# Causal attention on one core: the tail of one graph and the rows of the next in other places among the 16 items

## The reference

```python
h = _rmsnorm(x, ln1_w)
q = (h @ wq.T).reshape(Bx, Tx, NH, HD).transpose(0, 2, 1, 3)
k = (h @ wk.T).reshape(Bx, Tx, NKV, HD).transpose(0, 2, 1, 3)
v = (h @ wv.T).reshape(Bx, Tx, NKV, HD).transpose(0, 2, 1, 3)
q = q * cos + _rotate_half(q) * sin
k = k * cos + _rotate_half(k) * sin
scores = jnp.einsum('bhtd,bhsd->bhts', q, k) / jnp.sqrt(jnp.float32(HD))
scores = jnp.where(causal[None, None], scores, jnp.float32(-1e+30))
att = jax.nn.softmax(scores, axis=-1)
y = jnp.einsum('bhts,bhsd->bhtd', att, v).transpose(0, 2, 1, 3).reshape(Bx, Tx, Cx)
x = x + y @ wo.T
```

## Time and profile before

| | |
|---|---|
| time, median of 3 runs | 4995.22 us (4994.98 to 4999.32) |
| the profiled execution | 4982.11 us |
| its span | 4980.0 us |
| granted TensorE clock, mean | 0.818 |
| busy PE, DVE, ACT, POOL | 74%, 58%, 40%, 36% of the span |
| this stage | from 3842 to 4578 us of the span |

### The profile page before, as it was taken

One profiled execution on the slowest core, in us unless ns is written; L12 is line 12 of the kernel. 1 busy time (PEld: TensorE's weight loads), 2 busy tenths in 40 slices (PEclk: granted clock), 3 DMA queues, 4 the chain that ended last, 5 costly groups with the idle time before them and its releaser, 6 DMA issues. The chain is left out here.

```text
span 4980.0 us, 82349 instructions
## 1 busy us (share of the span) xinstructions
PE 3668.2 (74%) x24205; PEld 2239.0 (45%) x24205; DVE 2889.9 (58%) x10948; ACT 1986.3 (40%) x4974; POOL 1803.9 (36%) x2183
## 2 busy tenths in 40 slices
PE   3999985566666569999886766489667777764995
PEld 1333333444444323333364555357455444442663
DVE  5666655555555656666487867622377454543444
ACT  1666652222222236666432255334355433332221
POOL 3444421000000044445262136735545234342445
PEclk9999995555555579999998887699889988885997
DMA  4333319300000043333000022144431000001445
GB/s 125 115 113 103 103 50 419 143 0 0 0 0 0 0 130 106 111 106 95 13 0 1 1 89 76 38 133 148 145 101 52 1 9 14 14 17 45 130 130 162
DMA packets 237330, 378.21 MB, mean 76 GB/s; under 512 B 24832, under 2 KB 157056, under 8 KB 228672
## 3 DMA queue, kind: packets, MB, share of 16 engines
q1 hardware_dynamic: 218688, 337.44, 21.3%
q0 software_dynamic: 18432, 38.31, 2.2%
HBM read 210.70 MB, written 164.95 MB: 75 GB/s over the span
## 5 line engine op out<-in xcount | busy, mean ns | idle before, releaser
L1428 DVE CUSTOM_DVE_ANT_0 mha_seen<-mha_score,mha_mask 128x512 f32<-128x512 f32 x1024 | 686.6, 688 | 456.8 <-PE mha_score L1199 453.8
L1331 ACT ACTIVATE mha_prob<-mha_turned 128x512 f32<-128x512 f32 x1024 | 608.9, 601 | 491.8 <-PE mha_turned L1210 461.5
L1592 PE MATMUL lstm_gates<-lstm_h_part,lstm_w_part 128*128 128x16 f16 x4608 | 277.5, 179 | 338.2 <-DVE lstm_h_part L1779 338.2
L3071 POOL DMA_INDIRECT expert_rows<-expert_y,expert_target x320 | 307.1, 960 | 369.1 <-DVE expert_y L3217 155.4
L1199 PE MATMUL mha_score<-mha_k_rows,mha_q_rows 96*128 96x512 bf16 x1024 | 397.0, 390 | 56.9 <-DVE mha_low L1428 28.4
L1592 PEld LDWEIGHTS lstm_gates<-lstm_h_part,lstm_w_part 128*128 128x128 f16 x4608 | 215.7, 107 | 484.3 <-DVE lstm_h_part L1779 482.2
L1209 PE MATMUL mha_turned<-mha_maskT,core_ident_bf 128*128 128x512 bf16 x1024 | 393.3, 384 | 4.2 <-ACT mha_prob L1331 3.5
L1210 PE MATMUL mha_turned<-mha_q_rows,mha_k_rows 99*128 99x512 bf16 x1024 | 391.4, 382 | 0.0
L1542 POOL TENSOR_TENSOR core_mid<-lstm_hist,lstm_per_unit 128x128 f32 x64 | 29.3, 458 | 876.6 <-DVE lstm_hist L1780 876.6
L879 DVE CUSTOM_DVE_ANT_0 mha_prob<-mha_score,mha_mask 128x384 f32<-128x384 f32 (+3 forms) x256 | 125.0, 488 | 306.6 <-PE mha_score L518 222.2
L690 ACT ACTIVATE mha_prob<-mha_prob,mha_bias 128x384 f32<-128x384 f32 (+3 forms) x256 | 143.6, 561 | 361.3 <-DVE mha_bias L879 344.0
(11 more groups left out here) (559 smaller groups left out, 9055.4 us busy)
## 6 DMA issues: line engine op xcount, KB each, us to landing
routed_rows<-lstm_blank SPq DMA_DIRECT2D x66, 1056.0 KB, 27.0
core_params<-adj SPq DMA_DIRECT2D x32, 1024.0 KB, 5.6
gat_adj_raw<-adj SPq DMA_DIRECT2D x32, 1024.0 KB, 5.4
mha_q_rows<-split_rows SPq DMA_DIRECT2D x64, 384.0 KB, 4.3
mha_k_rows<-split_rows SPq DMA_DIRECT2D x64, 384.0 KB, 5.2
expert_x<-routed_rows SPq DMA_DIRECT2D x80, 264.0 KB
expert_w<-weights SPq DMA_DIRECT2D x80, 256.0 KB
combine_pair<-expert_rows SPq DMA_DIRECT2D x32, 512.0 KB, 4.9
```

The costliest lines, as they stand in the source:

```text
L1331: act.activation(prob[:, n % RING, :], turned[n % 2][:, :], ACT.Exp, scale=-1.0).then_inc(S["prob_ready"], 1)
L1428: dve.tensor_tensor_reduce(seen[n % 2][:, :], score[n % 2][:, :], mask[1 - s][:, t, :], 1.0, 3e38, ALU.add, ALU.min, low[g][:, t, j:j + 1] ...
L1592: return pe.matmul(out, w[:, g * P:(g + 1) * P], h_part[:, part, :], start=False, stop=stop, skip_group_check=True)
L3071: pool.indirect_dma_start(out=core.y_rows[NUMBER][:, :], out_offset=bass.IndirectOffsetOnAxis(ap=target[q][:, t:t + 1], axis=0), in_=y_buf ...
```

## The change

For this stage the steps get other items; `values` stays at 3.

| step | before | after |
|---|---|---|
| rows of the next graph | 9 | 0 |
| early (projections, rotations) | 10, 12 | 2, 4 |
| values of the graph before | 3 | 3 |
| back | 4 | 6 |
| ctx | 6 | 9 |
| out | 7 | 11 |
| v | 8, for this graph | 12, for the next graph |
| finish (DVE) | one piece each at 9 to 14 | two pieces each at 13, 14, 15 |

`v32` is held twice, so that v of the next graph can be made while values of this one are still to come; v of graph 0 is made ahead of the loop. POOL normalises the rows of graph b+1 behind its adds for graph b instead of ahead of its adds for b+1. The mask is one strip of 128 x 512, of which each tile reads another part, in place of 4 tiles of 512. Four small buffers that this form of the stage doesn't use are dropped.

```diff
-            at = {"values": 3, "back": 4, "ctx": 6, "out": 7, "v": 8, "rows": 9, "early": (10, 12)}
+            at = {"rows": 0, "early": (2, 4), "values": 3, "back": 6, "ctx": 9, "out": 11, "v": 12}
...
-        mask = [m.sb(f"mask{s}", [P, T, N], BF16) for s in range(1 if rope else 2)]
+        causal = m.sb("causal", [P, N], BF16) if rope else None
+        mask = [] if rope else [m.sb(f"mask{s}", [P, T, N], BF16) for s in range(2)]
...
-        v32 = m.sb("v32", [P, T, heads, 32])
+        v32 = [m.sb(f"v32{s}", [P, T, heads, 32]) for s in range(2)]
...
-                pool.memset(mask[0][:, :, :], 0.0).then_inc(S["adj_zero"], 1)
+                pool.memset(causal[:, :], 0.0).then_inc(S["adj_zero"], 1)
...
-                pool.affine_select(out=mask[0][:, :, :], in_=mask[0][:, :, :], compare_op=ALU.is_ge, fill=BIG, base=0,
-                                   pattern=[[P, T], [-1, N]], channel_multiplier=1).then_inc(S["adj_free"], 1)
+                pool.affine_select(out=causal[:, :], in_=causal[:, :], compare_op=ALU.is_ge, fill=BIG, base=(T - 1) * P,
+                                   pattern=[[-1, N]], channel_multiplier=1).then_inc(S["adj_free"], 1)
+
+            def normalise(b):
+
+                pool.wait_ge(S["xT_ready"], b + 1)
+                pool.tensor_tensor(xn[b % 2][:, :, :], core.mid[:, b], over_features(core.rms[:, b]), ALU.mult)\
+                    .then_inc(S["xn_ready"], 1)
...
+                    if b >= 4:
+                        pool.wait_ge(S["r_scaled"], (b - 2) // 2)
...
+            normalise(0)
             for b in range(B + 5):
                 if b < B:
                     graph(b, b % 2, first=b == 0)
+                if b + 1 < B:
+                    normalise(b + 1)
...
             def project_v(b):
 
+                pe.wait_ge(S["qk_ready"], 4 * b + 4 + 1)
...
-            def back_rows(b):
-
+            def back_rows(b, behind=True):
+
+                if behind:
+                    pe.wait_ge(S["qk_ready"], 4 * (b + 2) + 4 + 1)
...
-                    if n == at["v"]:
-                        project_v(b)
+                    if n == at["v"] and not last:
+                        project_v(b + 1)
...
-            dve.memset(v32[:, :, :, :], 0.0).then_inc(S["v32_set"], 1)
-            dve.wait_ge(S["v32_set"], 1)
...
-                        if 0 <= n - at["out"] - 2 < 6:
-                            finish(b - 1, n - at["out"] - 2)
-                    if n == at["v"] + 1:
-                        take_v(b)
+                        if n >= items - 3:
+                            finish(b - 1, 2 * (n - items + 3))
+                            finish(b - 1, 2 * (n - items + 3) + 1)
+                    if n == at["v"] + 1 and not last:
+                        take_v(b + 1, 1 - s)
```

More of the change, by code:

```diff
@@ L327, in mha_stage @@
         items = 4 * T * groups
-        rstd, shift = m.sb("rstd", [P, B, T]), m.sb("shift", [P, B, T])
-        scratch, term = m.sb("scratch", [P, B, T]), m.sb("term", [P, B, T])
+        rstd, shift, scratch, term = ((None,) * 4 if rope else
+                                      [m.sb(n, [P, B, T]) for n in ("rstd", "shift", "scratch", "term")])
         spare = Spare(core, k)
         adj_raw = None if rope else spare.sb([P, T, N], I32)
-        mask = [m.sb(f"mask{s}", [P, T, N], BF16) for s in range(1 if rope else 2)]
+        causal = m.sb("causal", [P, N], BF16) if rope else None
+        mask = [] if rope else [m.sb(f"mask{s}", [P, T, N], BF16) for s in range(2)]
         xn = [spare.sb([P, T, D]) for s in range(2)]
@@ L481, in project @@
                     pe.wait_ge(S["xT_ready"], b + 1 + 2)
-                    if rope:
-                        pe.wait_ge(S["batch_free"], b + 1)
+                    if rope and (not isinstance(b, int) or b):
+                        pe.wait_ge(S["batch_free"], b)
                 elif n == 2 and not rope:
@@ L528, in transposes, with values @@
                 last.then_inc(S["prob_free"], 1)
-            def values(b, g):
+            def values(b, g, s):
                 done = b * (items // 2) + 2 * T * (g + 1) + 1
@@ L539, in values @@
                         first = u * P if rope else 0
-                        last = pe.matmul(o_ps[g][32 * j:32 * j + 32, first:], v32[:, u, 4 * g + j, :], probT[:, j, u, first:],
+                        last = pe.matmul(o_ps[g][32 * j:32 * j + 32, first:], v32[s][:, u, 4 * g + j, :], probT[:, j, u, first:],
                                          start=(u == 0), stop=(u == T - 1))
                 last.then_inc(S["pv_done"], 1)
-            def back_rows(b):
+            def back_rows(b, behind=True):
+                if behind:
+                    pe.wait_ge(S["qk_ready"], 4 * (b + 2) + 4 + 1)
                 for g in range(groups):
@@ L567, in graph @@
                     if n == at["values"] and not first:
-                        values(b - 1, groups - 1)
+                        values(b - 1, groups - 1, 1 - s)
                     if n == at["values"] + 4 * T:
-                        values(b, 0)
+                        values(b, 0, s)
                     if n >= LAG:
@@ L576, in graph @@
                         if n == at["back"]:
-                            back_rows(b - 1)
+                            back_rows(b - 1, not last)
                         if n == at["ctx"]:
@@ L621, in _ @@
             early(0, 1)
+            project_v(0)
             if sym:
@@ L626, in _ @@
                 transposes(B - 1, n)
-            values(B - 1, groups - 1)
-            back_rows(B - 1)
+            values(B - 1, groups - 1, (B - 1) % 2)
+            back_rows(B - 1, False)
             turn_ctx(B - 1)
@@ L746, in _ @@
                 dve.wait_ge(S["adj_free"], 1)
-            else:
-                dve.memset(v32[:, :, :, head_dim:head_dim + 1], 1.0).then_inc(S["v32_set"], 1)
             def copy_probT(b, n):
@@ L774, in rotate, with take_v @@
                         .then_inc(S["qk_ready"], 1)
-            def take_v(b):
+            def take_v(b, s):
                 dve.wait_ge(S["v_done"], b + 1)
@@ L779, in take_v @@
                 if rope:
[L780 removed]
+                    dve.tensor_copy(v32[s][:, :, :, :], got).then_inc(S["v_ready"], 1)
                 else:
[L782 removed]
+                    dve.tensor_tensor(v32[s][:, :, :, 0:head_dim], got,
                                       bv.rearrange("p (h d) -> p h d", h=heads).unsqueeze(1).broadcast_to([P, T, heads, head_dim]),
@@ L876, in graph @@
                     dve.wait_ge(S["prob_free"], items * b + n + 1)
-                    allowed = mask[0] if rope else mask[s]
                     width = keys(t) * P
-                    dve.tensor_tensor_reduce(prob[:, n % PR, 0:width], score[n % 2][:, 0:width], allowed[:, t, 0:width], 1.0, 3e38,
+                    allowed = causal[:, N - width:N] if rope else mask[s][:, t, 0:width]
+                    dve.tensor_tensor_reduce(prob[:, n % PR, 0:width], score[n % 2][:, 0:width], allowed, 1.0, 3e38,
                                              ALU.add, ALU.min, bias[:, n % PR:n % PR + 1])\
@@ L910, in _ @@
                 rotate(0, 1)
+                take_v(0, 0)
             if sym:
```

3 lines of the change are left out of this document (removed).

## The result

| | before | after |
|---|---|---|
| time, median of 4 runs each | 4995.1 us (4991.2 to 4999.3) | 4879.8 us (4877.1 to 4882.6) |
| ratio, 95% interval | | 0.977 (0.975 to 0.979) |
| the profiled execution | 4982.1 us | 4878.5 us |

Faster by 115 us; 4870 us was forecast, with a range of 4835 to 4905, and 4879.8 lies in it. In the stage of the change the profiled executions give 112.7 us (from the first memset of DVE in the stage to the first operation of POOL in the next, 732.9 us before and 620.3 after). The profiled execution of after enters the stage some 10 us later, in parts that the change does not touch, so the profiled pair as a whole differs by only 103.6 us.

The account below looks back on a forecast made before the run. No engine was full; PE's in-order waits, the lower clock after them and the pause bound the stage. Savings of 29 (graphs 0-4), 90 (5-14), 2.5 (start) and 3 (graph 15) gave 124.5 us, ratio 0.975, 4870 us, range 4835 to 4905.

Parts of the forecast that it names:

- PE's seven stops: In graph 2, PE stops at seven places, 7.7 us in all, each step one or two items behind what it needs.
- The floor of 23.0 us: PE's work in graph 2: 35.7 us less 7.7 of waits and 5.0 lost to the lower clock.
- Graphs without routing: Graphs before the scatter begins: 27.3 us at full clock, 27.5 us with a partly low clock, against 35.7.
- next graph's first score waits for it: Items 12 to 15 hold 7.5 us of DVE work against PE's 4.5 + 0.9, costing 2.1 us a graph.
- Even graphs: Graphs 4, 6 to 14 with routing: DVE's extra work adds 1.3 + 3.2 us, giving 32 us, without the pause.
- pause: At values, ACT's copy comes 8.1 us after their start under a scatter, 2.9 without; 5.3 us stays in odd graphs.
- the lumps: Even graphs' 7.3 us of extra DVE work, at items 0 to 3 and 6 to 7, priced at 1.3 + 3.2 us.
- Odd graphs: Graphs 5, 7 to 13 with routing: 27.5 + 2.2 routing + 5.3 pause + 0.5 for scales = 35.5 us.
- B: Rival: from some point a scatter holds all PE work, not values alone; 50 us more, 4920 us; chance 0.25.
- A: Main case: as summed, odd graphs 35.5 us and even ones 32, total 4870 us, 4835 to 4905; chance 0.55.
- C: Rival: another order ahead of values frees the pause altogether, 26 us less and 10 from the clock: 4834; chance 0.13.
- Ports: `finish`'s DVE copy beside a scatter in odd graphs could wait about 1 us, five times: up to 5 us more.

Follow-up runs that it names:

- third group: Runs of the changed kernel (4782.3 us), with the spread (4785.6) and with spread plus late scatter (4790.6), beside the kernel before at 4909.3 us.
- late scatter: Changed kernel with POOL's scatter in odd rounds up to 15 waiting until PE's values are through: 4776.8 us in the first group, 4868.3 us in the second.
- second: Group with kernel before (4991.3 us), changed kernel (4878.5), late scatter (4868.3), and changed kernel with normalise back behind the scatter (4928.2).
- first group: Four edits of the changed kernel: scatters held back 4830.5 us, late scatter 4776.8, values head by head 4843.1, spread 4787.0; kernel before 4909.3.
- The spread: Changed kernel with ctx at item 8, out at 9, finish pieces over items 11 to 15: 4787.0 us in the first group, 4785.6 in the third group.

## Why the prediction was right, and which of its terms were off

**The kind of loss.** The forecast was that PE's seven stops go and that the clock comes back with them. Both show: graph 2 has 2.0 us of PE idle (7.6 before by the same count) and a clock of 1.00 (0.86). The floor of 23.0 us of PE's work measured 23.4.

**Start.** The first mask step comes 18.2 us behind DVE's first memset against 20.8: 2.6 us less, 2.5 forecast.

**Graphs without routing**, 27.5 us forecast, 25.8 and 25.4 measured. The term that failed is "next graph's first score waits for it", the 2.1 us of DVE's crowding in items 12 to 15: graphs 0 to 3 have 0.2 us of such a wait in all. (Its parts as the prediction lists them add up to 7.2 us and not 7.5, so that by its own prices it was 1.8.) Nearly all of PE's wait for L886 (39.0 us in the stage) lies in graphs with routing; in the third group 26.0 of the 26.7 us lie in even graphs, 4.0 to 4.4 us each. `back_rows` at 0.7 was near the 0.9 kept for it, ctx and out at 0.5 below the 1.3.

**Graph 3**, 30 forecast, 27.5 measured: the same term again.

**Even graphs**, 32 forecast, 33.6 measured, with DVE busy 27.5 of 33.4 us, 82%, and no pause, as forecast. That DVE is what PE meets there was right: in graph 6 of after 4.4 of PE's 6.5 idle us are waits for the mask, and in the third group one score alone waits up to 2.3 us. The price of the lumps was too low by more than the total shows. Over the 25.4 us of graph 2 an even graph takes 8.1 us more, where the prediction added 4.5 to a base that was 2 us too high.

**Odd graphs**, 35.5 forecast, 37.9 measured; this is the largest miss, 12 us over five graphs. Without a pause the changed kernel takes 27.5 there, so the sum's base of 30.2 (35.5 less the pause of 5.3) was 2.7 too high, and the scatters cost 37.9 - 27.5 = 10.4 us where the sum has 5.3. Graph 7 of after shows where they go. Its three windows run to the first mask step behind the pause, to that of item 9, and to graph 8:

```profile
4077.43:4090.54 13.11, 10.71 (x71) 5.77 (x69) 5.15 (x13) 5.51 (x17) 10.32 (x13) 1.00 0.11 37
4090.54:4099.44 8.90, 7.09 (x27) 5.85 (x28) 4.83 (x19) 5.18 (x18) 7.03 (x6) 0.51 0.03 9
4099.44:4115.15 15.71, 13.20 (x70) 9.02 (x68) 8.20 (x32) 6.66 (x20) 8.01 (x9) 0.95 0.10 34
```

and the same three in the changed kernel of the third group:

```profile
4043.87:4051.88 8.01, 7.51 (x57) 3.99 (x56) 5.14 (x13) 5.25 (x17) 6.49 (x9) 1.00 0.08 26
4051.88:4059.24 7.36, 6.64 (x45) 5.20 (x44) 4.83 (x18) 5.00 (x18) 4.69 (x5) 1.00 0.14 46
4059.24:4071.34 12.10, 11.51 (x68) 8.14 (x66) 8.20 (x34) 6.90 (x20) 10.43 (x11) 1.00 0.06 18
```

The pause at values costs 5.1 us (3.8 to 5.8 in the five odd graphs, 5.1 in the mean), so the 5.3 was right. Two terms were left out. Behind the pause PE goes on at its lower clock, 0.51 over 8.9 us, and the stretch takes 1.5 us longer (1.4 in the mean). The last 3.6 us (3.8 in the mean) are those of the even rounds' scatter in the middle of the odd graph. It stands where forecast, 22.4 to 32.3 us into it, and it holds PE's work too (DVE, then the scatter's first and last on POOL):

```profile
4104.88 0.69 DVE L886 CUSTOM_DVE_ANT_0 mha_prob<-mha_score,mha_causal 128x512 f32<-128x512 f32 x1 [2.24 <-PE mha_score L527]
...
4108.48 0.69 DVE L886 CUSTOM_DVE_ANT_0 mha_prob<-mha_score,mha_causal 128x512 f32<-128x512 f32 x1 [1.97 <-issue]
...
4111.44 0.69 DVE L886 CUSTOM_DVE_ANT_0 mha_prob<-mha_score,mha_causal 128x512 f32<-128x512 f32 x1 [1.32 <-remote]
...
4099.88 1.01 POOL L2370 DMA_INDIRECT routed_rows<-mha_r_rows,core_slot  x1 [0.15 <-issue]
...
4108.77 0.96 POOL L2370 DMA_INDIRECT routed_rows<-mha_r_rows,core_slot  x1 [0.30 <-issue]
```

The wide items stand 3.6 and 3.0 us apart there, and 2.0 in graph 3. So B's mechanism, a scatter that holds all of PE's work and not values alone, is what was measured, here and with the late scatter; its price, 8 us a second scatter, was not. The prediction names a scatter in mid graph that holds PE as a sign that it is wrong, and in this part it was: in the odd graphs 2.7 us of base too much stood against 5.1 us of scatter and clock too little, and graphs 0 to 4 were 7 us shorter than forecast. That A's time came out so near is in this part luck. C, another order that frees the pause, didn't happen: where the kernel before has the pause the change keeps it, and where the change has none neither has the kernel before.

**Graph 15**, 3 less forecast, 4.4 measured. **The sum** for the stage was 124.5 us less; measured 112.7 with the pause. By parts, between first mask steps, graphs 0 to 4 gave 35.2 us where 29 were forecast, graphs 5 to 14 gave 70.3 where 90 were. Without the pause, in the third group, the stage's first and last mask steps lie 126.8 us closer (587.6 and 460.8 us). That this is near 124.5 confirms nothing, since the sum had the pause in it.

**The pause and the change.** From the second to the third group, the time from first to last mask step falls by 53 us in the kernel before (640.8 to 587.6) and by 67 in the changed one (527.9 to 460.8). So the pause eats some 14 us of the gain. That the packed stage has more PE work under a scatter of the same length would explain it, and is argued, not shown. It is the difference between the ratios 0.978 and 0.974.

**Ports.** By the Trainium skill's "SBUF — State Buffer", section "Who interferes with whom", a DVE copy in a mode that uses both of its SBUF ports contends with GpSimd, and whichever comes first blocks the other for the whole instruction. By that `finish`'s copy could have waited for a DMA issue of POOL, or held it. In graph 7 of after it lies under the last issue of the second scatter and takes 0.42 us, as all 16 do, and the issue takes 0.96 like those before it. The Trainium skill's rule in the same section that PE and ACT never wait on anyone and a DMA contends with no engine agrees with the first and third group; in the second, PE's completions under the same scatter come late.

**What stays open.** What makes the pause come. It is steady through a group of runs and changes between groups. The records number the chips of the three groups 13, 4 and 4: if that number names one chip, the pause does not belong to the chip, which is what was supposed after the first group. The record doesn't tell what else the chip was doing, so a cause from outside the program is not excluded. Nor is it shown by what path an indirect DMA delays the semaphore that PE's last product sends; only that the product's own record is normal, and that the delay is bound to neither values nor their side by side products.

**The best version.** The late scatter gained 10 us with the pause (4868.3 against 4878.5), or 0.2%, about as little as can be told. Without it, it took 4776.8 beside a kernel before of 4909.3 us; the changed kernel took 4782.3 beside one of 4909.3 in another group; their ranges overlap, which is no difference that can be told. Its odd graphs take 28.1 us against 27.5 there, so it may cost some 3 us where there is no pause. The spread adds nothing to it: 4790.6 in the third group, 8 us more than the change alone.

## What to carry to other kernels

Put a step of an in-order engine two or three items behind what it needs, and each stop that goes can give back twice, once by itself and once by the clock (in graph 2, 5.6 us of PE's idle time and 4.7 us of its busy time). A pause takes twice in the same way, in graph 7 5.1 us and then 1.5. But count the narrow items by their time, since one item less between back, ctx and out brought the old wait back. When rows move to the front of a loop, move their producer ahead of whatever long list stands on its engine, here one normalise ahead of a scatter, worth 50 us in the group with the pause. And before an experiment is read, run the kernel before beside it: the same kernel differed by 82 us between groups of runs, more than most of the effects studied. In the profiled executions 53 us of this lie in this stage and 26 ahead of it, where the slower group has the pause as well.

## What the runs showed of the hardware

- An indirect DMA is issued every 1.26 us, and a list of eight can delay what waits for PE by up to 6 us (values up to 8.3 us instead of 2.4), while PE's records stay as they are. With one program, the changed kernel, it happened in every odd graph from 5 to 13 in one group of runs and in none in another. It isn't bound to this stage: in the same profiles 11 to 33 us of such waits stand ahead of it, all beside indirect DMAs or within 2 us of their end.
- Sixteen products of values written to four column groups in turn take 2.36 us, and 6.9 us one column group after the other.
- The granted clock over graph 2 is 1.00 in after, where PE's longest stop is 0.7 us, and 0.86 in the earlier trace rows, with stops of up to 1.8 us. Behind the pause in graph 7 of after it is 0.51 over 8.9 us, and 1.00 at the same place without a pause.
